# A graph layer's edge gathers: one semaphore per slot replaced by two halves that are waited for as a whole

## The reference

```python
h = relu(layernorm(x))
Qv, Ku = h @ W_Q.T, h @ W_K.T
score = einsum('md,md->m', Qv[dst], Ku[src]) / sqrt(128) * exp(-edge_dt)
# of each destination's edges the 16 of highest score are kept
w     = where(keep, exp(score - segment_max[dst]), 0)
alpha = w / segment_sum(w)[dst]
agg   = segment_sum(alpha[:, None] * (h[src] @ W_msg.T), dst)
out   = x + relu(h @ W_self.T + agg)
```

## Time and profile before

| | |
|---|---|
| three runs, median (lowest to highest) | 2120.7 us (2119.5 to 2123.81) |
| the profiled execution: its own time | 2119.5 us |
| its span in the profile | 2117.7 us |
| instructions | 47024 |
| GpSimd busy | 1517.5 us, 72% of the span |
| VectorE busy | 1466.1 us, 69% |
| TensorE matmul busy | 1431.0 us, 68% |
| ScalarE busy | 1020.9 us, 48% |
| gathers in the block loop | 1564 |

### The profile page before, as it was taken

One profiled execution on the slowest core, in us unless ns is written; L12 is line 12 of the kernel. 1 busy time (PEld: TensorE's weight loads), 2 busy tenths in 40 slices (PEclk: granted clock), 3 DMA queues, 4 the chain that ended last, 5 costly groups with the idle time before them and its releaser, 6 DMA issues. The chain is left out here.

```text
span 2117.7 us, 47024 instructions
## 1 busy us (share of the span) xinstructions
PE 1431.0 (68%) x15212; PEld 1326.2 (63%) x15213; DVE 1466.1 (69%) x4913; ACT 1020.9 (48%) x3179; POOL 1517.5 (72%) x1614
## 2 busy tenths in 40 slices
PE   0047777767677767767777777777666777777775
PEld 0036677667667667666666766766666766666664
DVE  3446776766776777677676776777767777767764
ACT  1525455544545545545554554554554554555443
POOL 2467777777777777777777777777777777777772
PEclk9988888887887878898888888888998887888887
DMA  7543333333333333333333333333333333333320
GB/s 181 187 124 86 96 100 100 88 97 92 95 98 101 89 94 100 97 88 101 94 92 98 100 88 96 100 89 97 100 93 89 101 92 92 101 98 89 97 73 24
DMA packets 118632, 207.48 MB, mean 98 GB/s; under 512 B 32423, under 2 KB 77635, under 8 KB 117613
## 3 DMA queue, kind: packets, MB, share of 16 engines
q0 software_dynamic: 50192, 103.42, 19.5%
q1 hardware_dynamic: 68190, 101.02, 15.0%
HBM read 187.87 MB, written 16.44 MB: 96 GB/s over the span
## 5 line engine op out<-in xcount | busy, mean ns | idle before, releaser
L597 POOL DMA_INDIRECT E<-H_table,idx x782 | 742.1, 949 | 270.7 <-issue 268.5
L597 POOL DMA_INDIRECT X<-H_table,idx x782 | 742.1, 949 | 241.8 <-issue 241.8
L982 ACT ACTIVATE X<-OT,w 128x125 f32<-128x125 bf16 x1792 | 530.0, 386 | 40.9 <-DVE w L860 40.5
L955 ACT ACTIVATE OT<-pT 128x512 bf16<-128x512 f32 (+1 forms) x500 | 274.6, 549 | 477.2 <-PE pT L1071 455.1
L1071 PE MATMUL pT<-identb,O 125*128 125x128 bf16 x1800 | 210.2, 242 | 288.4 <-DVE X L777 257.9
L1071 PEld LDWEIGHTS pT<-identb,O 125*128 125x128 bf16 x1800 | 135.4, 108 | 338.9 <-issue 279.2
L1060 PE MATMUL pG<-G,O 125*128 125x128 bf16 x3600 | 312.1, 249 | 0.0
L1060 PEld LDWEIGHTS pG<-G,O 125*128 125x128 bf16 x3600 | 273.2, 114 | 0.0
L782 DVE TENSOR_REDUCE s<-X 128x8 f32<-128x1024 f32 x200 | 268.5, 1343 | 0.0
L1096 PE MATMUL pU<-X 128*128 128x125 f32 x1800 | 230.0, 287 | 6.0 <-ACT X L982 4.8
L1096 PE MATMUL pU<-X,E 128*128 128x125 f32 x1800 | 227.4, 285 | 5.6 <-ACT X L982 5.5
(11 more groups left out here) (169 smaller groups left out, 2112.0 us busy)
## 6 DMA issues: line engine op xcount, KB each, us to landing
rawi<-D_table SPq DMA_DIRECT2D x50, 576.0 KB
ewt<-D_table SPq DMA_DIRECT2D x50, 576.0 KB
E<-H_table,idx POOLq DMA_INDIRECT x782
X<-H_table,idx POOLq DMA_INDIRECT x782
MR<-META_table SPq DMA_DIRECT2D x400, 9.0 KB
hb<-H_table SPq DMA_DIRECT2D x100, 62.5 KB
xb<-in_x SPq DMA_DIRECT2D x100, 62.5 KB
out<-ob SPq DMA_DIRECT2D x100, 62.5 KB
```

The lines of the kernel that those rows point to most:

```text
L597: return eng.indirect_dma_start(out=Et[q][:, t * 128:(t + 1) * 128], out_offset=None, in_=H, in_offset=bass.IndirectOffsetOnAxis(ap=idx[b ...
L955: AT.mark(eng.activation(OT[b % 3][:, q0[g]:q0[g] + GQ[g], :].rearrange("p t n -> p (t n)"), pT[:, 0:GQ[g] * 128], ACT.Copy), b, f"T{g}")
L982: last = eng.activation(weighted(c)[:, t * 128:t * 128 + NB], OT[c % 3][:, t, 0:NB], ACT.Copy, scale=w[:, t:t + 1])
```

## The change

The eight semaphores and the wait before each gather go. The block's gathers now fall into two halves. Tiles 1 to 6 (0 to 6 in the first block) raise `s_gp[0]`, tile 7 raises `s_gl`; then GpSimd waits until all of `s_gp[0]` has landed, tile 6 included. Tiles 8 to 14 raise `s_gp[1]`, tile 15 and, where there are any, tiles 16 and 17 raise `s_g[0]`; the optional tiles stand last in the block instead of first. At the block's end GpSimd waits until all of `s_gp[1]` has landed, tile 14 included. After tile 2 of the next block it waits for `s_g[0]` and raises `s_er`. VectorE's first two products wait for the first half, the third for tiles 8 to 14, the last two for `s_er`. ScalarE's `share` waits for `s_er` alone.

```diff
-        def landed(eng, b, t):
-            if b >= 0:
-                k = t % AHEAD
-                eng.wait_ge(s_gp[k], 16 * ((1 if k < 2 else 2) * b + t // AHEAD + (0 if k == 1 else 1)))
+        def but_last(b, k):
+            return 16 * (7 * (b + 1) - (b if k == 0 else 0))
...
                 AC.wait(eng, b - 4, "cp")
+                for t in range(1 if b else 0, HALF - 1):
+                    gather(b, t, s_gp[0])
+                    if t == 2 and b > 0:
+                        eng.wait_ge(s_g[0], total)
+                        eng.sem_inc(s_er, 1)
+                gather(b, HALF - 1, s_gl)
+                eng.wait_ge(s_gp[0], but_last(b, 0))
+                for t in range(HALF, SURE - 1):
+                    gather(b, t, s_gp[1])
+                gather(b, SURE - 1, s_g[0])
+                eng.reg_add(total, total, 16)
                 for t in range(SURE, T):
                     with eng.If(n > (t - 1) * 128):
-                        gather(b, t, s_g)
+                        gather(b, t, s_g[0])
                         eng.reg_add(total, total, 16)
-                eng.reg_add(total, total, 16)
-                for t in range(1 if b else 0, SURE):
-                    if t in (AHEAD, AHEAD + 1) and b > 0:
-                        landed(eng, b - 1, t)
-                    elif t >= AHEAD and t != AHEAD + 1:
-                        landed(eng, b, t - AHEAD)
-                    elif t < AHEAD and t != 1:
-                        landed(eng, b - 1, t + AHEAD)
-                    if t == 5:
-                        eng.wait_ge(s_g, total)
-                        eng.sem_inc(s_er, 1)
-                    gather(b, t, s_g if t == 1 else s_gp[t % AHEAD])
                 if b + 1 < B:
                     n = edges_of(b + 1)
+                eng.wait_ge(s_gp[1], but_last(b, 1))
+            eng.wait_ge(s_g[0], total)
+            eng.sem_inc(s_er, 1)
...
             def scores(b):
                 for g in range(5):
-                    if g == 0:
+                    if g < 2:
+                        eng.wait_ge(s_gp[0], but_last(b, 0))
+                        eng.wait_ge(s_gl, 16 * (b + 1))
+                    elif g == 2:
+                        eng.wait_ge(s_gp[1], but_last(b, 1))
+                    else:
                         eng.wait_ge(s_er, b + 1)
-                    for t in range(max(g0[g], 0 if b == 0 else 2), min(g0[g] + GG[g], SURE)):
-                        if t != 1:
-                            landed(eng, b, t)
...
             def share(b):
 
-                for t in range(SURE - AHEAD, SURE):
-                    landed(eng, b - 1, t)
                 eng.wait_ge(s_er, b)
```

More of the change, by code:

```diff
@@ L51, in gnn_kernel @@
     SURE = 16
-    AHEAD = 8
+    HALF = 8
     CH = [16, 16, 16, 14, 14, 12, 10]
@@ L222, in gnn_kernel @@
         s_st = [sem(f"s_st{q}") for q in range(2)]
-        s_g = sem("s_g")
+        s_g = [sem(f"s_g{q}") for q in range(2)]
         s_er = sem("s_er")
-        s_gp = [sem(f"s_gp{k}") for k in range(AHEAD)]
+        s_gp = [sem(f"s_gp{k}") for k in range(2)]
+        s_gl = sem("s_gl")
         s_relay = sem("s_relay")
@@ L593, in _, with gather @@
             eng.wait_ge(s_ht, 16 * nht)
-            def gather(b, t, signal):
+            def gather(b, t, landed):
                 q = b % 4
@@ L598, in gather @@
                     out=Et[q][:, t * 128:(t + 1) * 128], out_offset=None, in_=H,
-                    in_offset=bass.IndirectOffsetOnAxis(ap=idx[b % 3][:, t:t + 1], axis=0)).then_inc(signal, 16)
+                    in_offset=bass.IndirectOffsetOnAxis(ap=idx[b % 3][:, t:t + 1], axis=0)).then_inc(landed, 16)
             total = eng.alloc_register("total")
```

## The result

The changed kernel takes 2233.41 us (median of 4 runs, 2227.84 to 2236.42) against 2120.1 us (4 runs, 2119.13 to 2123.81): ratio 1.0529, 95% interval 1.0504 to 1.0553. Forecast were 2324 us with a range of 2250 to 2372. The sign and the place were right, the size was not.

The account below looks back on a forecast made before the run. GpSimd's nearly unbroken row of gathers was taken as the bound. 2119.5 + 100 (tile 8) + 62 (ends without tile 16) + 47 (ends with it) - 5 (old wait) + 0.5 (tail) = 2324 us, range 2250 to 2372.

Parts of the forecast that it names:

- GpSimd's row of gathers sets the time, one for one: GpSimd, first gather to last: it never stops but for some 13 us, so whatever lengthens its row delays the end equally.
- The old waits cost nothing: Waits of `landed` before gathers: already satisfied and hidden by the queue; removing 14 a block is worth nothing.
- the 5 us that were to go with the old wait at tile 5: Old wait ahead of tile 5, seen to break the pitch: its removal was to save 5 us of some 13.
- The restart of 0.72 us: GpSimd after a late landing: another 0.72 us pass before the next gather starts, since its queue has run empty.
- 100 + 62: Stalls: 1.0 us ahead of tile 8 in 100 blocks, 1.5 us at the end of 41 blocks without tile 16.
- The landings: Time from a gather's start to its landing: 2.50 us shortest, 5.19 long end; 2.78 taken for tile 6.
- Tile 3 and blocks with tile 16: Ends of 59 blocks with tile 16: waits for tile 14 and before tile 3 together stall 0.8 us, 47 us.
- Rival (1), quiet landings: Every awaited gather lands in 2.50 us, stalls total 102 us: 2216 us, all up to 2250 counted; chance 0.09.
- Rivals (2) to (4): (2) spread hits awaited gathers, 2377 us, 0.05; (3) fewer waits save, 1964, 0.03; (4) new waits stay hidden, 2114, 0.02.

Follow-up runs that it names:

- e7: Kernel before with every wait of `landed` made twice, on all engines; 3370.6 us, 1.0093 of the kernel before on that chip.
- m4: m2 plus an increment of an unused semaphore between the wait for tile 6 and tile 8's gather; 2513.9 us, gap ahead of tile 8 1.07 us.
- m2: Only the opening stage and the gathers, with the changed kernel's order and waits, all block calculation left out; 2516.4 us, gap ahead of tile 8 0.57 us.
- e3: Changed kernel plus an increment of an unused semaphore between the wait for tile 6 and tile 8's gather; 3319.6 us, 0.9896 of the kernel before.
- a1: Changed kernel, unedited, timed again on a chip where the kernel before took 3360.0 us; 3313.1 us, ratio 0.9861.
- e2: Changed kernel with the wait for tile 6 one gather earlier, ahead of tile 7; 2996.0 us, 0.8926 of the kernel before on that chip.
- e1: Changed kernel with the wait for tile 6 one gather later, ahead of tile 9; 3375.8 us, 1.0042 of the kernel before on that chip.
- b1: Kernel before, unchanged, run again with a trace; 3361.8 us, ratio 1.0004 to the kernel before on the same chip.

## Why the prediction was wrong, by its steps

**GpSimd's row of gathers sets the time, one for one: right.** The row grew by 118 us, the profiled execution by 119 (2238.3 against 2119.5).

**The old waits cost nothing: right.** The pitch between the gaps did not change, and doubling the old waits (e7) left the gaps at 0.30 to 0.32. Of the 5 us that were to go with the old wait at tile 5 about 1 went: 7 us of such gaps before, 6 elsewhere now.

**The restart of 0.72 us: wrong, and the main error.** It was measured at the one old wait that is followed by an increment, and carried over to waits directly ahead of a gather. There it is 0.26, in the changed kernel's own trace, and m4 against m2, e3 against a1 and e2 show what makes the difference. 0.46 us less in 141 stalls is 65 us of the 100 + 62.

**The landings: too long.** The gap ahead of tile 8 gives landing + restart = 2.50 + 0.36 = 2.86, so a landing of 2.60 where 2.78 was taken: 18 us. At the seam it is 2.50 + 0.61 - 0.26 = 2.85 against 3.28: 18 us more. Both were set between neighbouring rows, by VectorE's products, which can come later than the landing. The trace of the kernel before has tile 6's own landing signals: 2.65 us in the mean of the 73 blocks where all sixteen are recorded. It also has landings below the 2.50 that the prediction calls the shortest, down to 2.41 (median of 1079: 2.59). Restart and landing together are 101 us, the two terms' error (162 against 61).

**Tile 3 and blocks with tile 16: 47 us forecast, 59 measured** (6 + 53). Here the increment does stand between wait and gather, the restart was about as assumed (0.76 us behind L619), and the term was near; but some 14 us of it fell on blocks without tile 16, for which the prediction gave nothing because it counted the seam's stall of 1.5 us as cover, and that was 0.6.

**The sum.** 101 us less at these two places, 12 more at tile 3 and 4 of the 5 that didn't go turn the forecast's 2324 us into 2239; the profiled execution took 2238.3.

**Rival (1), quiet landings up to 2250 us,** has the right time for the wrong reason: landings were not at 2.50, the restart was short. Rivals (2) to (4) did not happen.

## What to carry to other kernels

Price a wait by landing + restart - cover, and look for each wait at what stands between it and the next instruction: a sequencer's own instruction in between costs half a microsecond that a wait carried by the gather itself does not. An engine that is never idle for want of work pays for every wait with too little cover, however long its sequencer runs ahead; one more gather between (e1) made it free. And a kernel at one engine's limit should be timed on more than one chip: the change that costs 5.3% on the first was no slower on another (a1, ratio 0.976 to 0.996 from two timings).

## What the runs showed of the hardware that I had not expected

A gather directly behind its only wait starts 0.26 us after the last landing signal, one with a sequencer's instruction between 0.8 us after it.

On six chips TensorE's matmuls, or the news of them, came late (13.2 us at L1084 in b1, the median) while GpSimd's gathers followed each other at 1.25 us, although the DMA engines were busy at 0.24 only, and TensorE caught up in breaks of 1.6 us. The kernel before took 3350 us there instead of 2120, one break a block took 10.4% off it, and two waits a block that only cost GpSimd time took 19.5% off. On one of these chips, with all other engines idle, the gathers ran at 1.38 us in the mean, with or without waits between them.
